# A two-layer graph kernel on one core: a chunk's semaphore is raised by a drain on TensorE in place of a product

## The chip, the cores and the metric
One core of one Trainium2 chip. The metric is the device time of the whole kernel in microseconds (us), the median over runs. TensorE is called PE in the profile (PEld its weight loads), VectorE DVE, ScalarE ACT, GpSimd POOL, SyncE SP.

## The reference
Two graph layers over 6250 nodes of 512 features and 106250 edges (`src`, `dst`), each followed by a layer norm:

```
x_l = x @ W_l.T + b_l                                   # layer 0
agg = segment_sum(x_l[src], dst);  deg = segment_sum(1, dst)
x   = layernorm(x + agg / max(deg, 1) + x @ W_r.T)
msg = h[dst] @ W_neigh.T + b_neigh                      # layer 1, h = x
neigh = segment_sum(msg, src) / max(deg, 1)
out = relu(h @ W_self.T + b_self + neigh)
x   = layernorm(x + layernorm(h + out) * gamma + beta)
```

The kernel sums the neighbours' rows first and multiplies by the weights afterwards, so the heavy part of each layer is: for each edge gather one row of 512 features and add it to the sum of its node.

## The kernel before
Nodes are cut into T = 49 tiles of 128. A layer's edges are cut into 928 chunks of 128 edges that all fall in one tile; two chunks make a group. For one chunk:

- POOL (`gathers`, L351 to L367) fetches the 128 rows from a table in HBM by an indirect DMA into one of GB = 8 slots of `rows`. A table row is a high and a low fp16 half with its scale. Before it reuses a slot it waits for `s_mm` of the chunk eight back (L363).
- DVE (`hot`, L563) builds `onehot`, the 128x128 matrix that says which row belongs to which node of the tile, once the rows have landed.
- PE (`sums`, L771) multiplies `onehot` with the two halves (two products of 512 columns) and with a column that counts edges (one product of 1 column). That last product raises `s_mm`.
- DVE (`add`, L572) adds a finished group from PSUM to `acc` in SBUF, some groups behind, after a wait for `s_mm` (L579), and raises `s_acc`. PE may start a group only when the sums of two groups back (layer 0) or four groups back (layer 1) have been added.

Chunks are handled in Python loops of U = 16 inside a hardware loop. In layer 1 the roles of `src` and `dst` are exchanged, so its edges must be sorted by the other end. That is done beside the first 832 chunks of layer 0, one column (`placed`) per chunk: DVE writes `spot` and `where` (`spots`, L585), ACT scales `spot` into `put1` and `put2` (`puts`, L851), and PE multiplies the two with `where` in four products of 464 columns (`place`, L747), the last of which raises `placed`. `spot`, `put` and `where` have PB = 4 slots, so DVE (L595) and ACT (L857) wait for `placed` of the column four back. On PE a chunk's column goes ahead of its sums.

The stages in order of time: preparation and the table of layer 0 (to about 520 us of the span), the 832 chunks with a placed column (to 1830), the last 96 chunks of layer 0 (to 1970), the projections and the norm of layer 0 (to 2350), the 928 chunks of layer 1 (to 3720), the projections and the norms of layer 1.

Of the kernel before, what the change touches and what calls it, by code (L numbers as in the profile page):

```python
# [18 lines left out]
def gnn_two_layers(nc, x, src, dst, w_l_t, b_l, w_r_t, w_self_t, b_self, w_neigh_t, b_neigh, gamma, beta, out):  # L19
# [12 lines left out]
    EC = -(-(-(-E // P)) // U) * U  # L32
# [18 lines left out]
    PB = 4  # L51
# [10 lines left out]
    with ctx:  # L62
# [122 lines left out]
        s_mm = sem("s_mm")  # L185
# [55 lines left out]
        @block.sync  # L241
        def _(sp):
            sp.wait_ge(s_pad, 3)
            for a, given in enumerate((src, dst)):
                sp.dma_start(edges[0:EFULL, a, :], given[0:EFULL * EC].rearrange("(p c) -> p c", c=EC)).then_inc(s_edges, 16)
                sp.dma_start(edges[EFULL:EFULL + 1, a, 0:EREST],
                             given[EFULL * EC:E].rearrange("(p c) -> p c", p=1)).then_inc(s_edges, 16)
            sp.dma_start(dst_next[0:EFULL, :], dst[1:EFULL * EC + 1].rearrange("(p c) -> p c", c=EC)).then_inc(s_edges, 16)
            sp.dma_start(dst_next[EFULL:EFULL + 1, 0:EREST - 1],
                         dst[EFULL * EC + 1:E].rearrange("(p c) -> p c", p=1)).then_inc(s_edges, 16)  # L250
            for a, given in enumerate((src, dst)):
                n = WP * WIN
                for b in range(WB - 1):
                    sp.dma_start(win_i[a][:, b, :], given[b * n:(b + 1) * n].rearrange("(p j) -> p j", j=WIN)).then_inc(s_wins, 16)
                sp.dma_start(win_i[a][0:WP - 1, WB - 1, :],
                             given[(WB - 1) * n:(NWIN - 1) * WIN].rearrange("(p j) -> p j", j=WIN)).then_inc(s_wins, 16)
                sp.dma_start(win_i[a][WP - 1:WP, WB - 1, 0:WREST],
                             given[(NWIN - 1) * WIN:E].rearrange("(p j) -> p j", p=1)).then_inc(s_wins, 16)
            for k in range(4):
                sp.dma_start(acc[:, k * XG:(k + 1) * XG, 0:D],  # L260
                             x[k * XG * P:(k + 1) * XG * P, :].rearrange("(t p) d -> p t d", p=P)).then_inc(s_x[k], 16)
            sp.dma_start(acc[0:LAST, T - 1, 0:D], x[(T - 1) * P:N, :]).then_inc(s_x[4], 16)

            with sp.Fori(0, T // BATCH) as i:
                for k in range(BATCH):
                    sp.wait_ge(s_high, BATCH * i + k + 1)
                    sp.wait_ge(s_low, BATCH * i + k + 1)
                    sp.wait_ge(s_tail, BATCH * i + k + 1)
                    sp.dma_start(tables[0][ds((BATCH * i + k) * P, P), :], rows[:, k, :]).then_inc(s_tab[k], 16)
            for layer in range(2):  # L270
                wa, wb = ((w_l_t, w_r_t), (w_neigh_t, w_self_t))[layer]
                if layer:
                    sp.wait_ge(s_proj, T)
                else:
                    sp.wait_ge(lists[1]["placed"], EC)
                    for n, a in enumerate((b_l, b_self, b_neigh, gamma, beta)):
                        sp.dma_start(vec[n], a.rearrange("(o d) -> o d", o=1).to_broadcast([P, D])).then_inc(s_vec, 16)
                sp.dma_start(w_a[:], wa.rearrange("(k p) n -> p k n", p=P)).then_inc(s_w, 16)
                sp.dma_start(w_b[:], wb.rearrange("(k p) n -> p k n", p=P)).then_inc(s_w, 16)
                source = (x, h_dram)[layer]  # L280
                target = (h_dram, out)[layer]

                def load(t, k, n=P):
                    sp.dma_start(own[0:n, k, :], source[ds(t * P, n), :] if not isinstance(t, int)
                                 else source[t * P:t * P + n, :]).then_inc(s_own[k], 16)

                def tile(t, k, load_next=True):
                    n = LAST if layer == 1 and isinstance(t, int) and t == T - 1 else P
                    sp.wait_ge(s_res, layer * T + t + 1)
                    rows_of = (lambda a: a[t * P:t * P + n, :]) if isinstance(t, int) else (lambda a: a[ds(t * P, n), :])  # L290
                    sp.dma_start(rows_of(target), res[0:n, k % 2, :]).then_inc(s_st[k % 2], 16)
                    if layer == 0:
                        sp.dma_start(rows_of(tables[1]), res_tab[0:n, k % 2, :]).then_inc(s_st[k % 2], 16)
                    if not isinstance(t, int) or t + OB < T:
                        last = isinstance(t, int) and t + OB == T - 1
                        load(t + OB, k, LAST if last and layer == 0 else P)

                sp.wait_ge(s_mm, chunk0(layer) + CHUNKS[layer])
                for t in range(OB):
                    load(t, t)  # L300
                over_tiles(sp, tile)
            for k in range(2):
                sp.wait_ge(s_st[k], stored(1, T - 1 - (T - 1 - k) % 2, k))
# [70 lines left out]
        def _(dve):  # L374
# [141 lines left out]
            def unpack(layer):  # L516

                s, n = lists[layer], CHUNKS[layer]
                dve.wait_ge(s["placed"], EC)
                halves = "p (h c) -> p h c"  # L520
                v2i, v2h = (flat[:, k * 1024:k * 1024 + n].bitcast(i32) for k in (0, 1))
                link(V.tensor_copy(v2i.rearrange(halves, h=2), ps[:, 2:4, 0:n // 2]))
                link(V.tensor_scalar(v2h, v2i, 8, None, ALU.arith_shift_right))
                link(V.scalar_tensor_tensor(g_idx[layer][:].rearrange(halves, h=2), ps[:, 0:2, 0:n // 2], 8.0,
                                            v2h.rearrange(halves, h=2), ALU.mult, ALU.add))
                link(V.tensor_scalar(v2h, v2i, 255, None, ALU.bitwise_and))
                link(V.tensor_scalar(g_loc[layer][:], v2h, -1.0, None, ALU.add))
# [57 lines left out]
            def spots(i, k, first):  # L585

                s, col = lists[1], U * i + k
                if k == 0:
                    if not first:
                        dve.wait_ge(s["where"], U * i)  # L590
                    V.tensor_copy(lo_ring[:], lo[:, ds(U * i, U)])
                    V.tensor_copy(hi_ring[:], hi[:, ds(U * i, U)]).then_inc(s_ring, 1)
                    dve.wait_ge(s_ring, i + 1)
                if not (first and k < PB):
                    dve.wait_ge(s["placed"], col - PB + 1)  # L595
                V.tensor_scalar(spot[:, k % PB, :], iota_node[:], lo_ring[:, k:k + 1], None,  # L596
                                ALU.is_equal).then_inc(s["spot"], 1)
                V.tensor_scalar(where[:, k % PB, 0:CHUNKS[1]], iota_chunk[:, 0:CHUNKS[1]], hi_ring[:, k:k + 1], None,  # L598
                                ALU.is_equal).then_inc(s["where"], 1)
# [108 lines left out]
        def _(pe):  # L708
# [38 lines left out]
            def place(layer, col, k, start=False, stop=False):  # L747
                s, half = lists[layer], CHUNKS[layer] // 2
                pe.wait_ge(s["where"], col + 1)
                if layer:  # L750
                    pe.wait_ge(s["put"], col + 1)
                for n, put in enumerate((put1, put2)):
                    for b in range(2):
                        last = mm(ps[:, 2 * n + b, 0:half], put[:, k % PB, :],
                                  where[:, k % PB, b * half:(b + 1) * half], start=start, stop=stop)
                last.then_inc(s["placed"], 1)

            pe.wait_ge(s_flag, 3)
            flag = pe.value_load(unsorted[0:1, 0:1], min_val=0, max_val=1)
# [11 lines left out]
            def sums(layer, i, first=False, placing=None):  # L771
                g = GROUP[layer]
                for k in range(U):
# [7 lines left out]
                    if k % g == 0 and not (first and q < 2):  # L781
# [4 lines left out]
                    mm(ps[:, bank, :], lhs, row[:, D:2 * D], start=False, stop=stop)  # L786

                    mm(ps[:, bank + 1, 0:1], lhs, row[:, 2 * D + 2:2 * D + 4].bitcast(bf16)[:, 0:1],
                       start=start, stop=stop).then_inc(s_mm, 1)

            for layer in range(2):
                iters = CHUNKS[layer] // U
# [42 lines left out]
        def _(act):  # L835
# [15 lines left out]
            def puts(c, first=False):  # L851
                s = lists[1]
                for k in range(PB):
                    col = PB * c + k
                    act.wait_ge(s["spot"], col + 1)
                    if not first:
                        act.wait_ge(s["placed"], col - PB + 1)  # L857
                    nc.scalar.activation(put1[:, k, :], spot[:, k, :], ACT.Copy, scale=val1[:, ds(col, 1)])  # L858
                    nc.scalar.activation(put2[:, k, :], spot[:, k, :], ACT.Copy,  # L859
                                         scale=val2[:, ds(col, 1)]).then_inc(s["put"], 1)  # L860
# [59 lines left out]
```

## Time and profile before

| | us |
|---|---|
| median of 3 runs | 4253.43 (4247.24 to 4258.62) |
| the profiled execution | 4222.63 |
| its span | 4220.8 |
| PE busy in the span | 2795.4 |
| DVE busy | 2605.4 |
| POOL busy | 1896.1 |
| ACT busy | 813.8 |

The span runs from the first to the last instruction of the profiled execution. Shares of busy time are averages over stages with different limits; each stage has to be read by itself.

### The profile page before, as it was taken

The page shows a single profiled execution, that of the slowest core. Times are in us where ns is not written, and L with a number is a line of the kernel's source. Part 1 is how long each engine was busy: PE and PEld are TensorE (multiplying, and loading weights), DVE is VectorE, ACT ScalarE, POOL GpSimd, SP SyncE. Part 2 cuts the span into 40 slices and gives each one's busy share as a digit, 9 for nine tenths or more (in the row PEclk, how much of TensorE's full clock was granted, in tenths as well). Part 3 has the DMA queues.
Part 4 walks back from the last instruction along what each step waited for, and adds up shares of the span by engine and source line. Part 5 has one row for each costly group of instructions (what it writes and reads, how often), then busy time and mean ns, then how long its engine had stood idle before and what let it go on. Part 6 is the DMA issues. An engine that isn't in the chain of part 4 may idle for free.

```text
span 4220.8 us, 57125 instructions
## 1 busy us (share of the span) xinstructions
PE 2795.4 (66%) x11308; PEld 1186.1 (28%) x11308; DVE 2605.4 (62%) x6523; ACT 813.8 (19%) x2156; POOL 1896.1 (45%) x2073
## 2 busy tenths in 40 slices
PE   1000088888888888866999655555555555568887
PEld 1000033333333433322554211111111111124443
DVE  3878877777777777754555444444444444448887
ACT  0300044444444444410222000000000000002222
POOL 0600066666666666664000366666666666630000
PEclk9555599999999999976999766666566665669999
DMA  3300066666666666664333566666666666661111
GB/s 141 123 0 0 21 169 165 170 165 167 167 169 166 168 167 167 168 202 137 102 103 98 160 178 173 179 179 179 177 178 174 180 177 177 172 115 60 55 60 50
DMA packets 201222, 586.38 MB, mean 139 GB/s; under 512 B 34672, under 2 KB 35502, under 8 KB 201196
## 3 DMA queue, kind: packets, MB, share of 16 engines
q0 software_dynamic: 148480, 488.56, 42.6%
q1 hardware_dynamic: 52716, 97.53, 7.1%
q8 instruction: 10, 0.16, 0.0%
q14 instruction: 16, 0.13, 0.0%
HBM read 534.51 MB, written 51.44 MB: 139 GB/s over the span
## 4 chain that ended last, share of the span: by engine, by line
PE 38%; DVE 19%; issue 19%; DMA 8%; DVEq 6%; POOL 2%; another core or an unknown queue 2%; ACT 2%; SPq 2%; POOLq 0%; ACTq 0%
PE ps L710 37%; DMA rows<-table,idx_ring 7%; DVEq L576 4%; DVE acc L583 3%; DVE onehot L569 2%; POOL rows L364 2%; DVE flat L501 2%; DVE flat L502 1%; DVE flat L503 1%; DVE where L598 1%; PE ps L812 1%; DVE st L658 1%; DVE spot L596 1%; PE ps L815 1%
## 5 line engine op out<-in xcount | busy, mean ns | idle before, releaser
L364 POOL DMA_INDIRECT rows<-table,idx_ring x1856 | 1793.8, 966 | 1394.7 <-issue 462.6
L710 PE MATMUL ps<-rows,onehot 128*128 128x512 f16 (+1 forms) x5568 | 1393.7, 381 | 758.0 <-DVE onehot L569 346.3
L583 DVE TENSOR_TENSOR acc<-acc,ps 128x513 f32 x928 | 638.2, 688 | 830.5 <-issue 353.7
L710 PE MATMUL ps<-where,put 128*128 128x464 f16 x3328 | 805.5, 365 | 348.8 <-ACT put L859 291.4
L710 PEld LDWEIGHTS ps<-rows,onehot 128*128 128x128 bf16 x5568 | 526.5, 111 | 1650.1 <-issue 888.2
L569 DVE TENSOR_SCALAR onehot<-iota_node,loc_ring,rows 128x128 bf16<-128x128 f16 x1856 | 586.4, 323 | 297.6 <-DMA rows<-table,idx_ring 253.1
L858 ACT ACTIVATE put<-spot,flat 128x128 f16<-128x128 f16 x832 | 334.1, 402 | 1091.7 <-DVE spot L596 860.7
L710 PEld LDWEIGHTS ps<-where,put 128*128 128x128 f16 x3328 | 268.1, 98 | 659.2 <-issue 351.8
L598 DVE TENSOR_SCALAR where<-iota_chunk,hi_ring 128x928 f16<-128x928 f16 x832 | 378.8, 455 | 0.0
L872 ACT ACTIVATE flat<-acc,rdeg 128x512 f32 (+1 forms) x98 | 69.4, 710 | 1551.2 <-DVE rdeg L647 1547.6
L710 PE MATMUL ps<-w_a,flat 128*128 128x512 f32 x784 | 356.0, 597 | 0.1
L710 PE MATMUL ps<-w_b,flat 128*128 128x512 f32 x784 | 352.4, 592 | 0.0
L859 ACT ACTIVATE put<-spot,flat 128x128 f16<-128x128 f16 x832 | 321.0, 386 | 0.6 <-issue 0.6
L596 DVE TENSOR_SCALAR spot<-iota_node,lo_ring 128x128 f16<-128x128 f16 x832 | 210.0, 252 | 28.0 <-PE ps L710 17.2
L710 PEld LDWEIGHTS ps<-w_b,flat 128*128 128x128 f32 x784 | 149.0, 190 | 187.5 <-issue 187.5
L345 POOL COPY acc<-zeros 128x513 f32 (+1 forms) x49 | 34.4, 703 | 344.3 <-ACT flat L872 344.3
L710 PEld LDWEIGHTS ps<-w_a,flat 128*128 128x128 f32 x784 | 142.8, 192 | 144.0 <-issue 143.1
L891 ACT ACTIVATE sd<-mv,eps 128x1 f32<-128x1 f32 x147 | 43.3, 295 | 626.8 <-DVE mv L663 626.8
L679 DVE SCALAR_TENSOR_TENSOR flat<-where,has,ps 128x512 f32<-128x512 f32 x49 | 36.6, 747 | 133.1 <-PE ps L710 133.1
L710 PE MATMUL ps<-totals,ones 128*128 128x49 f32 x2 | 0.7, 430 | 160.3 <-DVE flat L480 160.3
L658 DVE BATCH_NORM_STATS2 st<-flat 128x6 f32<-128x512 f32 x147 | 102.1, 695 | 5.0
L812 PE MATMUL ps<-ident,flat 128*128 128x128 f32 x392 | 62.3, 283 | 59.9 <-ACT flat L881 49.1
(131 smaller groups left out, 1361.9 us busy)
## 6 DMA issues: line engine op xcount, KB each, us to landing
rows<-table,idx_ring POOLq DMA_INDIRECT x1856
table<-rows SPq DMA_DIRECT2D x98, 257.0 KB, 3.2
h_scratch<-rows SPq DMA_DIRECT2D x49, 256.0 KB, 2.0
rows<-h_scratch SPq DMA_DIRECT2D x49, 256.0 KB, 2.7
acc<-in_x SPq DMA_DIRECT2D x4, 3072.0 KB, 23.5
rows<-in_x SPq DMA_DIRECT2D x48, 256.0 KB, 3.2
out<-rows SPq DMA_DIRECT2D x48, 256.0 KB, 2.0
w_a<-in_w_l_t SPq DMA_DIRECT2D x1, 1024.0 KB
```

The source lines that it names most:

```text
L364: nc.gpsimd.indirect_dma_start(out=rows[:, k % GB, :], out_offset=None, in_=tables[layer][:, :], in_offset=bass.IndirectOffsetOnAxis(ap=id ...
L501: link(V.tensor_tensor_scan(run, mask[:], mask[:], base[:, ds(b, 1)], ALU.add, ALU.bypass))
L569: V.tensor_scalar(onehot[:, k % SB, :], iota_node[:], loc_ring[:, k:k + 1], rows[:, k % GB, 2 * D:2 * D + 2].bitcast(f32), ALU.is_equal, A ...
L576: tile = dve.value_load(g_tile[layer][0:1, ds(U // g * i + q, 1)], min_val=0, max_val=T - 1)
L583: V.tensor_tensor(tile_acc, tile_acc, part, ALU.add).then_inc(s_acc, 1)
L596: V.tensor_scalar(spot[:, k % PB, :], iota_node[:], lo_ring[:, k:k + 1], None, ALU.is_equal).then_inc(s["spot"], 1)
L598: V.tensor_scalar(where[:, k % PB, 0:CHUNKS[1]], iota_chunk[:, 0:CHUNKS[1]], hi_ring[:, k:k + 1], None, ALU.is_equal).then_inc(s["where"], 1)
L658: V.bn_stats(st[:], dest).then_inc(v, 1)
L710: return nc.tensor.matmul(*args, skip_group_check=True, **kw)
L812: nc.tensor.transpose(ps[:, 0, j * P:(j + 1) * P], mean_nb[:, k % 2, j * P:(j + 1) * P], ident[:])
L858: nc.scalar.activation(put1[:, k, :], spot[:, k, :], ACT.Copy, scale=val1[:, ds(col, 1)])
L859: nc.scalar.activation(put2[:, k, :], spot[:, k, :], ACT.Copy, scale=val2[:, ds(col, 1)]).then_inc(s["put"], 1)
```

## The change
A product no longer raises `s_mm`. After the three products of a chunk PE executes a drain, and the drain raises `s_mm`. Since PE's stream has the placed column of a chunk ahead of its sums, the drain stands for that column too: `placed` of layer 1's list is dropped, and DVE, ACT and SP wait for `s_mm` in its place, with the same number. No product, vector instruction or transfer is added, dropped or put in another order; 1856 drains are added. The branch for unsorted edges (`bin_column`), which these inputs do not take, keeps its own `placed`.

```diff
@@ sync
-                    sp.wait_ge(lists[1]["placed"], EC)
+                    sp.wait_ge(s_mm, EC)
@@ vector, unpack
-                dve.wait_ge(s["placed"], EC)
+                if layer:
+                    dve.wait_ge(s_mm, EC)
+                else:
+                    dve.wait_ge(s["placed"], EC)
@@ vector, spots
                 if not (first and k < PB):
-                    dve.wait_ge(s["placed"], col - PB + 1)
+                    dve.wait_ge(s_mm, col - PB + 1)
@@ tensor, place
-                last.then_inc(s["placed"], 1)
+                if layer == 0:
+                    last.then_inc(s["placed"], 1)
@@ tensor, sums
                     mm(ps[:, bank + 1, 0:1], lhs, row[:, 2 * D + 2:2 * D + 4].bitcast(bf16)[:, 0:1],
-                       start=start, stop=stop).then_inc(s_mm, 1)
+                       start=start, stop=stop)
+                    nc.tensor.drain().then_inc(s_mm, 1)
@@ scalar, puts
                     if not first:
-                        act.wait_ge(s["placed"], col - PB + 1)
+                        act.wait_ge(s_mm, col - PB + 1)
```

## Rows read from the trace of the kernel before

**Rows 1.** Windows, one row per stage: busy us and count of each engine, clock, DMA
```profile
core 0: us, PE busy (x) PEld busy (x) DVE busy (x) ACT busy (x) POOL busy (x), PEclk, DMA share, GB/s
530.00:1820.00 1290.00, 1094.26 (x5739) 500.14 (x5738) 957.30 (x3183) 569.82 (x1644) 812.96 (x821) 0.98 0.62 167
1840.00:1950.00 110.00, 64.08 (x223) 21.69 (x222) 48.60 (x131) 0.00 (x0) 68.79 (x73) 0.59 0.66 193
2430.00:3700.00 1270.00, 733.39 (x2568) 238.27 (x2567) 557.69 (x1496) 0.00 (x0) 810.11 (x857) 0.62 0.64 177
```

**Rows 2.** Groups by line and form, window 2430 to 3700 (layer 1's chunks)
```profile
L364 POOL DMA_INDIRECT rows<-table,idx_ring x857 | 810.5, 946 | 460.1 <-issue 212.0 <-PE ps L710 140.5 <-remote 107.6
L710 PE MATMUL ps<-rows,onehot 128*128 128x1 bf16 x856 | 169.5, 198 | 0.0
```

**Rows 3.** Timeline of layer 0 with columns, the steady rhythm: start, us, engine, instruction
```profile
1506.06 0.94 PE L710 MATMUL ps<-where,put 128*128 128x464 f16 x4
1506.84 0.60 PE L710 MATMUL ps<-rows,onehot 128*128 128x512 f16 x3
1507.30 0.94 PE L710 MATMUL ps<-where,put 128*128 128x464 f16 x4
```

**Rows 4.** Timeline of layer 0 with columns, a stop of all engines
```profile
1496.03 0.60 PE L710 MATMUL ps<-rows,onehot 128*128 128x512 f16 x3
...
1496.49 0.94 PE L710 MATMUL ps<-where,put 128*128 128x464 f16 x4
1496.83 0.94 POOL L364 DMA_INDIRECT rows<-table,idx_ring  x1 [0.37 <-issue]
1499.11 0.69 DVE L583 TENSOR_TENSOR acc<-acc,ps 128x513 f32 x1 [3.50 <-remote]
...
1499.74 0.94 POOL L364 DMA_INDIRECT rows<-table,idx_ring  x1 [1.98 <-remote]
...
1499.86 0.61 PE L710 MATMUL ps<-rows,onehot 128*128 128x512 f16 x2 [2.42 <-DVE acc L583]
```

**Rows 5.** Timeline of layer 1's chunks, another such stop
```profile
2607.09 0.98 POOL L364 DMA_INDIRECT rows<-table,idx_ring  x1 [0.30 <-issue]
...
2608.57 0.31 DVE L569 TENSOR_SCALAR onehot<-iota_node,loc_ring,rows 128x128 bf16<-128x128 f16 x1
...
2608.93 0.61 PE L710 MATMUL ps<-rows,onehot 128*128 128x512 f16 x3 [0.95 <-issue]
2609.17 0.94 POOL L364 DMA_INDIRECT rows<-table,idx_ring  x1 [1.10 <-PE ps L710]
...
2611.89 1.03 PE L710 MATMUL ps<-rows,onehot 128*128 128x512 f16 x3 [2.35 <-DVE onehot L569]
2612.05 0.94 POOL L364 DMA_INDIRECT rows<-table,idx_ring  x1 [1.93 <-remote]
```

**Rows 6.** Timeline of layer 0's norm: a product ends, DVE starts
```profile
2049.79 2.31 PE L710 MATMUL ps<-w_b,flat 128*128 128x512 f32 x5
...
2052.25 0.75 DVE L679 SCALAR_TENSOR_TENSOR flat<-where,has,ps 128x512 f32<-128x512 f32 x1 [2.60 <-PE ps L710]
```

**Rows 7.** Waits, window 530 to 1820: us in total, times, longest
```profile
POOL rows L364 <- PE ps L710: 221.8, 143, 2.4
DVE acc L583 <- PE ps L710: 156.3, 108, 3.4
DVE acc L583 <- remote: 91.4, 30, 3.7
```

**Rows 8.** Chain that ended last, by line, windows 530 to 1830 and 2360 to 3710
```profile
by line: PE ps L710 57.5%; issue 12.3%; DVE acc L583 6.2%; another core or an unknown queue 5.2%; DVE where L598 3.8%; DVEq L576 3.5%; DVE onehot L569 3.4%; DVE spot L596 2.6%; ACT put L859 1.9%; DVEq L583 0.5%; DVE idx_ring L560 0.4%; ACT 
by line: issue 34.3%; PE ps L710 19.7%; DMA rows<-table,idx_ring 17.7%; DVEq L576 7.8%; POOL rows L364 6.5%; DVE onehot L569 3.6%; DVE acc L583 3.5%; another core or an unknown queue 1.9%; DVEq L583 1.2%; DVEq L578 0.9%; DVEq L579 0.7%; DVE
```

**Rows 9.** The page's second part: granted clock of PE in 40 slices
```profile
PEclk9555599999999999976999766666566665669999
```

## The prediction
> **What bounds the kernel now.** I read the windows by stage first, then the timelines of two stretches, then the waits and the chain. The windows [rows 1] give three stages that the change touches. With placed columns, 821 gathers start in 1290 us, so a chunk takes 1.571 us; in the last 96 chunks of layer 0 it takes 110/73 = 1.51 us; in layer 1 1270/857 = 1.482 us. No engine is full in any of them: PE is busy 85% of the first and 58% of the last, POOL 63% and 64%, DVE 74% and 44%, and the DMA engines 62 to 66%.
>
> Two floors can be read. POOL needs 0.946 us for a gather in layer 1 [rows 2] and 0.99 with columns (812.96 us for 821 [rows 1]), and its queue adds 0.30 us between two when nothing else is waited for (the gather at 2607.09 [rows 5]). That makes about 1.25 and 1.29 us. PE, in the steady rhythm with columns, goes from one chunk's first placing product at 1506.06 to the next one's at 1507.30 [rows 3]: 1.24 us, with the clock at its upper level (0.98 granted [rows 1]). So 0.28 to 0.33 us of every chunk with columns, and 0.23 us of every chunk of layer 1, are stops.
>
> The stops have a form that the timelines show. At 1497.43 (1496.49 + 0.94) PE has ended all it may do; it waits for a DVE add. That add waits for a product that PE finished before 1497.43, yet it starts only at 1499.11, after 3.50 us of idle whose end the profile puts down to "remote", that is, to nothing that it knows. POOL's last gather ended at 1497.77 and it waits till 1499.74 [rows 4]. For 1.3 us nobody works, and the one event that can end it is PE's semaphore. In layer 1 PE's last product ends at 2609.54 (2608.93 + 0.61), and POOL, free since 2610.11, starts its next gather at 2612.05, again by "remote" [rows 5]. In the norm, where POOL gathers nothing, the same kind of signal is prompt: products that end at 2052.10 release DVE at 2052.25 [rows 6]. I read this as: **while gathers run, the semaphore that a product raises can arrive 1 to 3 us after the product has ended**, and DVE's signals to PE do not (an onehot that ends at 2608.88 lets PE start at 2608.93 [rows 5]). With columns POOL and DVE wait 222 + 156 + 91 us for PE or "remote" [rows 7], in part at the same time; in layer 1 POOL alone waits 140.5 + 107.6 us [rows 2].
>
> **The change part by part.** *The drain's price on PE.* No row has a drain in such a place. PE must let the last product end before it starts the next. That product is the one-column one; a mean of 0.198 us in layer 1 [rows 2], and today the next product starts about 0.03 us behind it (the seven products start at seven places in 1.24 us: four by 0.195, two by 0.215, the rest of 0.03 is the one-column product [rows 3]). Lost overlap: 0.17 - 0.03 = 0.14 us at the upper clock, taking the one-column product at 0.17 there, which is an estimate from 0.198 for a mostly lower clock. After it the queue must start again; a semaphore-to-product restart takes 0.05 us [rows 5], and the drain itself and the wait instruction behind it are of that size each. Estimate 0.25 us per chunk; bounds 0.14 (the overlap alone) and 0.45 (0.14 plus a restart as slow as POOL's 0.30).
>
> *What hides it.* With columns PE's rhythm becomes 1.24 + 0.25 = 1.49, still under the 1.571 of today. In layer 1, where the clock is mostly at the lower level (0.62 granted [rows 1]), PE needs 733.39/857 = 0.86 us per chunk, with a drain some 1.1, under POOL's 1.25. So the drain is covered in both, if the stops go away; if they stay, PE's share of the chain (57.5% [rows 8]) grows with it.
>
> *The drain's semaphore.* The new signal is raised by PE's queue after the engine is empty, and not by the product. I take it to be prompt. That is the choice on which the forecast stands, and no row shows it; what speaks for it is that products pile up behind the late signal (PE works on for up to three chunks after the product that the add waits for), so it is the message that is late and not the work, and that the signals of the other engines are not late in the same microseconds [rows 4, 5].
>
> A page of the Trainium skill can be laid beside this. Perfetto Trace Analysis, sections "Tensor Engine Instruction" and "Sequencer-only Instruction (DRAIN, etc)", lets a product's update be pushed once PSUM has acknowledged the writes, and a drain's by the sequencer: another route, which is what the forecast needs, though no run here shows whether it is a faster one. PSUM — Partial Sum Buffer, section "Engine vs sequencer instructions", says to put the increment on the product itself, since it fires on completion, and that a drain waits for the engine to go fully idle. By that rule nothing is late today and the drain only costs (the first rival below). The norm agrees with it, the stop at 1499.11 does not.
>
> *The dropped signal.* DVE's `spots` and ACT's `puts` now wait for the whole chunk four back and not for its column alone: 0.46 us later (1507.30 - 1506.84 [rows 3]) plus the drain. Behind that wait in DVE stand onehot and the add, behind ACT's the next `put`. The slots are four chunks deep, 6 us, so I cost it at nothing; if DVE's lead over PE is gone it is up to 0.5 us per stop. SP's weight loads start 0.5 us later, beside the 96 chunks: nothing. One update fewer per chunk on PE: nothing, no row prices it.
>
> *The sum, chosen.* With columns a chunk goes from 1.571 to 1.53 (PE's 1.49 and a rest for DVE's and POOL's own unevenness): 832 x 0.04 = 33 us saved. Bounds: with a drain at 0.14, PE 1.38, chunk 1.42, 125 saved; at 0.45, PE 1.69, chunk 1.69, 100 lost. Last 96 chunks: half of the way from 1.51 to 1.25: 12 saved. Layer 1: the way from 1.482 to POOL's 1.25 is 0.23; I take half, since DVE's queue and the landings stop POOL too (DVEq, issue and DMA hold most of the chain [rows 8]): 928 x 0.12 = 111 saved; bounds 0 and 0.21, 195. Norms and preparation: 0. Together 33 + 12 + 111 = 156 us. The profiled execution took 4222.6, so 4067 by its own time; the median of the runs lies 31 us above it (4253.4), so I give 4097 as the time. Ends of this case: -340 and about 0.
>
> *The clock.* It is at the upper level while PE works without pause and mostly at the lower one in layer 1 [rows 9]. Here PE's products per microsecond do not fall if the chunk does not get longer, so I give it nothing.
>
> **The rivals.**
> 1. *The drain mends nothing.* Its semaphore is as late as the product's, or the product's was never late. The stops stay, and each chunk on PE's part of the chain pays the drain: 0.575 x 1300 = 748 us [rows 8] are 603 chunks of 1.24, times 0.25 = 150; in layer 1 0.197 x 1350 = 266 us, about 300 chunks of 0.86, of which a fall of 0.15 each would be 45. Some is given back because PE runs dry less often; I take 150 in all: 4253 + 150 = 4403. It decides once lateness gives back less than about 0.1 us per chunk. For it: the rhythm has only 0.33 us of slack. Against it: signals of other engines come in time.
> 2. *The drain itself is held until the late message is out.* Then PE can't work on in a stop: per stop (138 waits of DVE with columns [rows 7], about 130 of POOL in layer 1) two chunks are done after it and not in it: 138 x 2 x 1.24 = 342, 130 x 0.86 = 112: 4253 + 450 = 4700. Against it: one would expect the message, not the engine, to be stuck.
> 3. *It comes out even.* The drain costs 0.45 us, with columns 100 us are lost, layer 1 gives 111 back: 4253 - 11 = 4242. Or what ends the stops is a gather's landing and not PE's semaphore, and the drains are all covered: also about 4250. Against: PE waits in [rows 4] with all its inputs there but the add.
>
> **How the numbers follow.** Forecast 0.51, rival 1 0.27, rival 2 0.12, rival 3 0.10. Within 0.3% (13 us, about what a measurement of this kernel can tell from no change) is half of rival 3 and a little of the edges: 0.06. Faster: the forecast and a fifth of rival 3, 0.53. Slower: 0.41. The time is that of the likeliest, 4097; its own range is 3990 to 4210. The range that leaves 0.1 below and the second rival above reaches from 3990 to 4450.
>
> **What would show it.** In the profile after: stops ended by "remote" gone from DVE's add and POOL's gather with columns and in layer 1; gathers per microsecond in layer 1 up, 1.36 us per chunk; with columns PE's rhythm 1.49 and not 1.24 and few waits of PE for the add. The forecast is wrong if "remote" waits stay (rival 1), if PE stands between a product's end and the next start for over 1 us again and again (rival 2), or if the rhythm with columns is over 1.57 (rival 3).

## The result, and the profile after

| | before | after |
|---|---|---|
| median of 4 runs, us | 4254.04 (4247.24 to 4258.62) | 4426.99 (4418.61 to 4428.11) |
| the profiled execution | 4222.63 | 4428.11 |
| its span | 4220.8 | 4426.3 |

The changed kernel takes 1.0404 of the time of before [1.0385, 1.0423]: 173 us more, where 156 us less were forecast. The profile of before (4222.63) lies outside the range of its four runs and inside that of chip 2 below (4214.22 to 4224.43), and the record doesn't say on which chip it was taken. So the two profiles differ by 205.5 us where the medians differ by 173, and up to 33 us of what follows by stage need not be the change's. The profiles put the loss in the stages that the change touches. First the page of the changed kernel: its busy times, the granted clock (answers to [rows 9]) and, from the fifth part, the two groups that wait longest for PE's queue.

```profile
PE 3019.8 (68%) x11308; PEld 1192.7 (27%) x11308; DVE 2708.9 (61%) x6523; ACT 813.2 (18%) x2156; POOL 1869.2 (42%) x2073
...
PEclk9555699999999999995799955555555555559999
...
L364 POOL DMA_INDIRECT rows<-table,idx_ring x1856 | 1766.8, 952 | 1624.4 <-PEq L794 833.5
...
L586 DVE TENSOR_TENSOR acc<-acc,ps 128x513 f32 x928 | 640.1, 690 | 786.5 <-PEq L794 545.0
```

L794 is the drain. Then the windows by stage (they answer to [rows 1]): busy us and count of each engine, clock, DMA share.

```profile
540.00:1900.00 1360.00, 1074.85 (x5401) 475.15 (x5400) 986.89 (x2990) 535.01 (x1544) 740.82 (x772) 0.99 0.55 149
1950.00:2040.00 90.00, 64.51 (x269) 23.61 (x268) 50.13 (x145) 14.55 (x42) 53.92 (x58) 0.76 0.69 205
2560.00:3870.00 1310.00, 886.90 (x2569) 241.13 (x2570) 572.20 (x1499) 0.00 (x0) 809.36 (x857) 0.50 0.62 172
```

Gathers per window give the time of a chunk: with placed columns 1360/772 = 1.762 us (was 1.571), in layer 1 1310/857 = 1.529 (was 1.482), in the last 96 chunks of layer 0 90/58 = 1.55 (was 1.51). Times 832, 928 and 96 that is +159, +43 and +4 us: 206 us, the difference of the spans (205.5). The other stages lose nothing.

The waits of the stage with columns (us in total, times, longest; answers to [rows 7]):

```profile
POOL rows L364 <- PEq L794: 540.0, 654, 2.4
DVE acc L586 <- PEq L794: 309.1, 339, 3.8
```

"Remote" is gone, as forecast. But the two engines now wait more often, for PE's queue. The timeline of the same place as [rows 3 and 4] shows why:

```profile
1490.61 0.94 PE L713 MATMUL ps<-where,put 128*128 128x464 f16 x4 [0.33 <-ACT put L864]
...
1491.09 0.94 POOL L364 DMA_INDIRECT rows<-table,idx_ring  x1 [0.81 <-PEq L794]
...
1491.39 0.60 PE L713 MATMUL ps<-rows,onehot 128*128 128x512 f16 x3
...
1492.16 0.69 DVE L586 TENSOR_TENSOR acc<-acc,ps 128x513 f32 x1 [0.97 <-PEq L794]
...
1492.32 0.94 PE L713 MATMUL ps<-where,put 128*128 128x464 f16 x4 [0.32 <-issue]
...
1492.80 0.94 POOL L364 DMA_INDIRECT rows<-table,idx_ring  x1 [0.76 <-PEq L794]
```

PE's rhythm is 1492.32 - 1490.61 = 1.71 us where it was 1.24. The stops of 2 to 3 us are gone, and every chunk has a pause of 0.33 us instead. The trace's records of PE's queue split the 0.49 us from the start of the one-column product to the next product's start (medians): 0.19 until the drain has ended, 0.10 more until a register instruction starts, 0.09 until the wait on the next chunk's inputs, 0.08 until the weight load, 0.03 until the product. Without the drain the whole way took 0.03. So **a drain costs 0.46 us a chunk with columns**, and 0.30 of it comes after the drain has ended, while the queue starts again from empty.

In layer 1 (records again) the next product starts 0.43 to 0.55 us after the one-column product's start, where before it took about 0.07, and there most chunks are held by it: chunks follow each other every 1.25 or 1.35 us on PE, at or above POOL's 1.25. And a new kind of stop stands there (timeline, answers to [rows 5]):

```profile
2988.88 1.03 PE L713 MATMUL ps<-rows,onehot 128*128 128x512 f16 x3 [0.22 <-issue]
...
2991.39 0.13 PEld L713 LDWEIGHTS ps<-rows,onehot 128*128 128x128 bf16 x2 [1.97 <-issue]
2991.40 1.03 PE L713 MATMUL ps<-rows,onehot 128*128 128x512 f16 x3 [1.49 <-issue]
2991.60 0.69 DVE L586 TENSOR_TENSOR acc<-acc,ps 128x513 f32 x1 [0.69 <-PEq L794]
...
2991.86 0.94 POOL L364 DMA_INDIRECT rows<-table,idx_ring  x1 [1.46 <-PEq L794]
```

The products end at 2989.91, and the next chunk's inputs have been there for long (in the median a onehot is done 6.9 us ahead of its last product). Still PE, DVE and POOL start only at 2991.4 or after: by its record the drain ended 1.38 us after the one-column product's start. It was held. In the records of 870 chunks of layer 1, 15% of the drains end over 0.4 us after the one-column product's start (normally 0.24; at the 95th percentile 1.99), 178 us too much in all. With columns it is 0.9% of them.

### The profile page after: what moved, and what is told of

The parts are those of the page before. It is cut to its first block, busy times and chain, and to the rows that moved or that the text cites. A ratio compares the mean times of both kernels' runs of the same rounds, so it can differ in the third digit from the quotient of the medians.

```text
span 4426.3 us, 58981 instructions
## 1 busy us (share of the span) xinstructions
PE 3019.8 (68%) x11308; PEld 1192.7 (27%) x11308; DVE 2708.9 (61%) x6523; ACT 813.2 (18%) x2156; POOL 1869.2 (42%) x2073
## 4 chain that ended last, share of the span: by engine, by line
issue 33%; PEldq 21%; DVE 17%; PE 13%; PEld 6%; DMA 3%; ACT 3%; DVEq 2%; SPq 2%; ACTq 1%; POOL 0%; POOLq 0%
PEldq L794 19%; PE ps L713 11%; PEld ps L713 6%; DVE acc L586 2%; DVE flat L501 2%; DMA rows<-table,idx_ring 2%; ACT put L864 2%; DVE spot L599 2%; DVE flat L502 1%; DVE flat L503 1%; DVE where L601 1%; PE ps L817 1%; DVE st L661 1%; PE ps L820 1%; DVE onehot L572 1%
## 5 line engine op out<-in xcount | busy, mean ns | idle before, releaser
L364 POOL DMA_INDIRECT rows<-table,idx_ring x1856 | 1766.8, 952 | 1624.4 <-PEq L794 833.5
L713 PE MATMUL ps<-rows,onehot 128*128 128x512 f16 (+1 forms) x5568 | 1562.7, 406 | 529.2 <-issue 445.8
L713 PE MATMUL ps<-where,put 128*128 128x464 f16 x3328 | 794.3, 361 | 558.5 <-ACT put L864 357.3
L572 DVE TENSOR_SCALAR onehot<-iota_node,loc_ring,rows 128x128 bf16<-128x128 f16 x1856 | 623.1, 338 | 441.2 <-DMA rows<-table,idx_ring 423.1
L601 DVE TENSOR_SCALAR where<-iota_chunk,hi_ring 128x928 f16<-128x928 f16 x832 | 394.2, 474 | 0.0
```

The costliest lines, as they stand in the source:

```text
L364: nc.gpsimd.indirect_dma_start(out=rows[:, k % GB, :], out_offset=None, in_=tables[layer][:, :], in_offset=bass.IndirectOffsetOnAxis(ap=id ...
L572: V.tensor_scalar(onehot[:, k % SB, :], iota_node[:], loc_ring[:, k:k + 1], rows[:, k % GB, 2 * D:2 * D + 2].bitcast(f32), ALU.is_equal, A ...
L713: return nc.tensor.matmul(*args, skip_group_check=True, **kw)
```

## The experiments

Chips differ, and this has to be known for all that follows. On the chip of the result and on chips 14, 13 and 2 (it may be one of them, the record gives it no number) the kernel before takes 4218 to 4255 us; on chips 12, 7, 0 and 1 it takes 3780 to 3785. The ratios of times are all within one chip. I read each trace's records of semaphore updates against the ends of the products that raise them. "Late" is over 60 ns behind. The shares are of the updates that are on record: in chip 12's trace all of them are, in the profile of before 684 of 820 with columns and 648 of 856 in layer 1. An update is set against the last product that ended ahead of it, so the real lateness can only be larger.

```
s_mm of the kernel before / without `placed`   late with columns   late in layer 1   us per chunk
the profile of before                          72%                 56%               1.571 / 1.482
chip 12 (e2)                                   0                   0                 1.306 / 1.259
chip 2 (e18)                                   78%                 62%               1.577 / 1.480
```

In the profile of before half of the recorded signals come over 0.68 us late with columns (worst 2.6 us), in layer 1 the worst is 6.0. In the same windows DVE's and ACT's signals come 8 to 13 ns after the end, as on chip 12 (only half to three quarters of them are on record, though), and PE's come within 15 ns in the norm of layer 0. So the forecast's reading of the stops held: where signals are prompt, the very same program takes 11% less time, and its chunks run at POOL's floor of 1.25 to 1.3 us.

One thing beside the late signals also differs, and the forecast had no term for it. In layer 1 of the profile of before 286 instructions of DVE's own queue, nearly all of which otherwise take 0.02 to 0.06 us, took about 0.7, 178 us in all (289 and 179 us on chip 2, none on chip 12). DVE's queue stands on the chain of that stage [rows 8], so a part of layer 1's stops is DVE's and not PE's; no run parts the two. In the changed kernel 45 are left.

**The drain without its signal.** Before, with a bare drain behind each chunk's products, which raises nothing.

```diff
                        start=start, stop=stop).then_inc(s_mm, 1)
+                    nc.tensor.drain()
```

> The kernel before, with a drain that raises nothing behind the three products of every chunk; the one-column product still raises s_mm and the placed column its own semaphore. It asks whether the route of the signal matters or only the pause and the slower pace that the drain brings. Theory A (the route: a signal raised by a drain is prompt, one raised by a product is late while gathers run): POOL's start after the end of the one-column product of eight chunks back stays spread over 2.4 to 5.6 us as before, and the time is above that of the changed kernel, 4440 to 4550 us, since the drain's price (0.46 us per chunk with columns) is paid and the lateness too. Theory B (the pause: lateness goes because PE stops after each chunk and POOL no longer runs back to back with columns): the same 0.80 us as after the change, and the time of the changed kernel, 4410 to 4440 us.

> The kernel of the first experiment again (a drain that raises nothing behind every chunk; the products raise the semaphores). Where signals are prompt it must equal the changed kernel within 0.3%, as the drain's pause is all that counts. On a chip with lateness it parts route from pause: by theory A (route) the products' signals stay late and it is slower than the changed kernel by 1% or more, by theory B (pause and slower pace) equal to it.

Chip 12: 4178.59 us against 3780.48, 1.1052 [1.1034, 1.1071]. Chip 7: 4185.11 against 3784.94, 1.1058 [1.104, 1.1077]. A chunk takes 1.720 us with columns and 1.319 in layer 1 (1.306 and 1.259 without): 832 x 0.414 + 928 x 0.060 = 400 of the 398 us. The price of the drain is there with no change in who signals. The second expectation was missed: it put this kernel within 0.3% of the changed one, which takes 0.6% more (4210.96, below). Whether the pause or the signal's route cures lateness could not be told on chips that have none.

**The dropped signal alone.** The products raise `s_mm` as before; `placed` is dropped and its waits go to `s_mm`.

```diff
-                    dve.wait_ge(s["placed"], col - PB + 1)
+                    dve.wait_ge(s_mm, col - PB + 1)
...
-                last.then_inc(s["placed"], 1)
+                if layer == 0:
+                    last.then_inc(s["placed"], 1)
...
-                        act.wait_ge(s["placed"], col - PB + 1)
+                        act.wait_ge(s_mm, col - PB + 1)
```

> One part of the change alone: the semaphore placed is dropped and DVE, ACT and SP wait for s_mm in its place, but s_mm is still raised by the one-column product and there is no drain. Theory A (what costs is the drain on PE): within 0.5% of the kernel before, 4235 to 4275 us. Theory C (the later release of the placed column's slots costs): slower by 1 to 2%, 4300 us or more. Theory D (PE's signals are late because there are two per chunk to deliver): faster, 4150 to 4220 us, with fewer waits that nothing explains.

> The part of the change without drains (placed dropped, the one-column product raises s_mm), again, for a chip with lateness. Theory D (fewer signals of PE, less lateness): faster than the kernel before by 1% or more there, with fewer late signals than 72%. Theory A (the number does not matter): within 1%, with 60 to 80% of the signals with columns late. On a chip without lateness 1.000 again.

> placed dropped alone, a third time, for the same purpose. On a chip with lateness, theory D: faster by 1% or more; theory A: within 1%. On a chip without it 1.000 again.

1.000 [0.999, 1.0009] on chip 12, 0.9999 [0.9989, 1.0008] on chip 1, and on chip 2, where signals are late, 1.0006 [0.9996, 1.0016]. Half as many updates per chunk with columns leave 78% of the rest late. The windows of chip 12's run, with columns and in layer 1, show what the program does with prompt signals. The second window runs past the last gather at 3305 us, so its 714 gathers took 905 us, 1.27 each:

```profile
560.00:1600.00 1040.00, 1004.29 (x5578) 485.77 (x5576) 939.96 (x3089) 551.89 (x1592) 794.74 (x797) 1.00 0.73 202
...
2400.00:3400.00 1000.00, 723.95 (x2365) 232.47 (x2364) 544.36 (x1360) 19.70 (x43) 674.75 (x714) 0.63 0.71 193
```

**Fewer drains.** One drain per group of two chunks, which raises `s_mm` by 2; `placed` is dropped here too, as in all that follows on `s_mm`.

```diff
+                    if k % g == g - 1:
+                        nc.tensor.drain().then_inc(s_mm, g)
```

> The changed kernel, with one drain per group of two chunks that raises s_mm by 2, so half as many drains. If the drain's price is 0.46 us on PE with columns and 0.36 to 0.45 in layer 1, half of it goes: with columns PE's rhythm goes from 1.70 to 1.47 us per chunk, in layer 1 from 1.30 to about 1.08. Theory A (PE's rhythm is the bound after the change in both stages): 150 to 190 us less with columns and 60 to 130 us less in layer 1, in all 4130 to 4220 us, under the kernel before. Theory E (in layer 1 it is the held drains and not PE's rhythm): only the part with columns is won, 4240 to 4280 us.

> The kernel with one drain per group of two chunks, again, for a chip with lateness. PE's rhythm with columns is 1.47 us per chunk, so gathers are again issued more closely. Theory P: as the pace comes near that of the gathers lateness returns in part; 4180 to 4280 us, about the kernel before. Theory A' (half the drains give the whole relief): 4050 to 4180 us, under the kernel before. On a chip without lateness 3940 us again.

Chip 12: 3939.04, 1.042 [1.0403, 1.0437]; 1.500 us with columns, 1.261 in layer 1, where it costs nothing. Half of the drains cost about half: 0.19 of the 0.43 of the changed kernel (1.734 against 1.306). Chip 13, where signals are late: 4341.55 against 4254.75, one run each, above both of its expectations; 1.680 and 1.520. By the records 47% of its drains with columns end over 0.4 us after the one-column product's start (none on chip 12), 125 us too much over 760 chunks, 0.165 a chunk: that and chip 12's 1.500 are 1.665 of the 1.680. In layer 1 it is 35%. In the changed kernel, with a drain after every chunk, 0.9% and 15% were held: in these two kernels, the more products stand between two pauses, the more drains are held.

**Drains in layer 0 alone.** The change as it is, but in layer 1 the one-column product raises `s_mm`.

```diff
+                    (nc.tensor.drain() if layer == 0 else count).then_inc(s_mm, 1)
```

> Drains in layer 0 alone; in layer 1 the one-column product raises s_mm as before. It parts the loss by layer. From the traces (1.571 to 1.762 us per chunk with columns, 1.482 to 1.529 in layer 1) 160 us of the loss belong to layer 0 and 44 to layer 1 of the profiled execution: 4254 + 130 to 165 = 4385 to 4420 us, with layer 1 at 1.48 us per chunk. A rival: the traces of single executions mislead and layer 1 is where the loss is: 4300 us or less.

Chip 12: 4137.15, 1.0942 [1.0924, 1.096]; 1.734 us with columns, 1.260 in layer 1. Of the change's loss there some 357 us are layer 0's.

**The change itself where signals are prompt, and with a second drain.**

```diff
                        start=start, stop=stop)
+                    nc.tensor.drain()
                     nc.tensor.drain().then_inc(s_mm, 1)
```

> The changed kernel itself, once more. The first four experiments ran on a chip on which the kernel before takes 3780 us and not 4254, and on which every signal of a product arrives within 20 ns. Theory F (a drain costs PE 0.46 us per chunk everywhere, and it is only the lateness, where a chip has it, that pays a part back): on a chip without lateness the ratio is 1.10 to 1.11, about 4180 us against 3780; on one with lateness it is 1.04 again. A rival: the ratio is 1.04 on every chip, and the difference of the chips is something that meets both kernels alike.

> The changed kernel with a second drain, which raises nothing, ahead of the one that raises s_mm. It splits the 0.46 us: what is the wait for the last product to end is paid once, what is the drain's own handling is paid twice. If the wait and the restart of the weight load and product are most of it: PE's rhythm with columns goes up by 0.02 to 0.10 us, the time by 20 to 100 us over the changed kernel on the same chip. If it is the drain's own handling: by 0.2 us or more, 200 us or more.

Chip 7: the change takes 4210.96 against 3784.94, 1.1128 [1.111, 1.1147], 426 us more; 1.734 and 1.334 us a chunk, and no drain longer than 0.24 us. That the drain carries the signal costs 26 us over the silent one (4185.11). Two drains take 4349.54, 1.1498 [1.1479, 1.1517]: the second adds 0.076 us from product to product, and 1.812 and 1.412 us a chunk (0.078 each). So of the first one's 0.46 only some 0.08 is what one more drain adds; the rest, lost overlap and the restart, is paid once per pause.

**No drain, one signal per group.** `last` is the one-column product.

```diff
+                    if k % g == g - 1:
+                        last.then_inc(s_mm, g)
```

> No drain; placed dropped; the one-column product of the second chunk of each group raises s_mm by 2 and that of the first chunk nothing: a quarter of the signals with columns, half in layer 1. Theory D (late signals come of too many): on a chip with lateness faster than before by 1% or more, without lateness within 0.5% or up to 1% slower, since slots come free two at a time. Theory A (number does not matter): within 1% or slower on either.

> One signal per group, raised by 2 by the one-column product of the group's second chunk, no drain, placed dropped, again, for a chip with lateness: a quarter of the signals with columns and half in layer 1. Theory D: 1 to 4% faster than the kernel before there. Theory A: equal, or 1 to 3% slower, since a late signal now holds back two slots. On a chip without lateness 0.999 again.

> One signal per group by the second chunk's product, no drain, placed dropped, a third time, to find it on a chip with lateness (the kernel before above 4200 us). Theory D (fewer signals, less lateness): 1 to 4% faster than the kernel before there. Theory A: equal, or 1 to 3% slower, since a late signal holds back two slots. On a chip without lateness 0.998 again.

0.9989 [0.998, 0.9999] on chip 7, 0.9984 [0.9974, 0.9993] on chip 1, and 1.0028 [1.0016, 1.0039] on chip 2, where 78% of the recorded signals with columns are still late. With lateness it is no cure, without it it gives 4 or 5 us. So the number of signals is not the cause.

**Memory traffic of its own.** SP copies pieces of `x` inside HBM beside the chunks of both layers, one after the other; the kernel's result doesn't use them.

```diff
+            def traffic(done):
+                for i in range(150):
+                    sp.dma_start(bg[0:512, :], x[0:512, :]).then_inc(s_bg, 16)
+                    sp.wait_ge(s_bg, 16 * (i + done + 1))
```

> The kernel before with foreign traffic: SP copies the first 512 rows of x (1 MB) to a scratch in HBM, 150 times beside layer 0's chunks and 150 times beside layer 1's, one at a time. It asks whether a product's signal becomes late when the memory is loaded by someone else, on a chip where it is prompt. Theory G (lateness comes from load on the memory and the DMA engines): signals of products in the chunk stages arrive up to microseconds after the end, waits that nothing explains appear, the time is over 4100 us. Theory H (load on them does nothing to the signals; the lateness comes from elsewhere on the chip): the gathers get slower, the chunks wait for landings, and every signal of a product still arrives within 20 ns of its end; 3850 to 4300 us.

> The same with small copies: 64 rows (128 KB), 300 times in each layer, one at a time. Theory G: a small number of late signals, 3800 to 3950 us. Theory H: none, and the time within 1% of the kernel before on the same chip, as the gathers leave the DMA engines a quarter of their time.

> The changed kernel with the traffic of 1 MB copies. Theory G: the drains give back a part of the lateness, and it stands at a ratio of 1.02 to 1.07 to the kernel before with the same traffic, not at 1.11. Theory H: where both wait for landings the drains' price is partly covered by them, the ratio lies between 1.03 and 1.10 with no late signal and no drain held longer than 0.27 us after the last product's start.

One run each on chip 0. With 1 MB pieces before takes 3928.78 (3782.29 without), 1.420 and 1.322 us a chunk at a DMA share of 0.92 and 330 GB/s, and not one product signal is late; with pieces of 64 rows the time does not move (3782.29). The changed kernel with the large pieces takes 4235.01 (1.078 of before with them) and no drain is held. On this chip more traffic than on any late one does not make PE's signals late; on a late chip it was not tried.

**The silent drain where signals are late.** The kernel of the first experiment on chip 14.

> The kernel with a drain that raises nothing, a third time, to find it on a chip on which the kernel before takes about 4254 us. There, by theory A (route), the signals of its products are late as before and it takes 4440 us or more; by theory B (the pause and the slower pace), its signals are prompt with columns and it takes 4380 to 4440 us. On a chip on which the kernel before takes 3780 us it must take 4180 us again and tells nothing new.

4397.29 against 4218.34, one run each (1.042, as the change itself). Product signals are now late in 1.2% of the chunks with columns and 20.8% of those of layer 1, although they take the old route; and 15.3% of layer 1's drains are held, some 180 us in all, as in the changed kernel. So it is the pause that makes signals prompt, and not the drain's route. This trace has both records for 561 chunks of layer 1. Where the drain was held (115), the product's signal was late in 114, in two thirds of them 33 ns ahead of the drain's end, in the others 0.7 or 1.4 us ahead; where it was not (446), in 2, and the signal again 32 to 34 ns ahead of the drain's end. **A drain is held where the product's signal is late, and it never ended before that signal.** Most of these drains end with the signal; the rest are held for one or two more steps of 0.7 us, the same length that DVE's queue shows. Two chunks of its timeline with columns, for PE:

```profile
1490.93 0.94 PE L710 MATMUL ps<-where,put 128*128 128x464 f16 x4 [0.31 <-issue]
...
1491.71 0.60 PE L710 MATMUL ps<-rows,onehot 128*128 128x512 f16 x3
...
1492.62 0.94 PE L710 MATMUL ps<-where,put 128*128 128x464 f16 x4 [0.31 <-issue]
```

**A slower PE without a pause.** In place of a drain, four extra products of 512 columns ahead of each group's first one, with columns only; the first real product overwrites what they leave.

```diff
+                    if placing is not None and start:
+                        for _ in range(4):
+                            mm(ps[:, bank, :], lhs, row[:, 0:D], start=True, stop=False)
```

> The kernel before, without drains and with placed, with four extra products of 512 columns in each group of layer 0's chunks with columns (they write what the group's first product then overwrites, so nothing else changes). PE's rhythm there goes from 1.24 to 1.24 + 2 x 0.215 = 1.67 us per chunk, near the drains' 1.70, but PE never pauses. Theory P (pace: signals are late where gathers are issued back to back, and a slower chunk alone ends it): on a chip with lateness less than 10% of the signals with columns come late, a chunk takes 1.67 to 1.75 us, the time is 4300 to 4400 us. Theory Q (pause: PE must empty for its signals to get out): over half of the signals stay late with columns and a chunk takes 1.8 us or more, 4450 us or more. On a chip without lateness both give 1.68 to 1.70 us per chunk and 4090 to 4120 us.

```profile
540.00:1840.00 1300.00, 1300.00 (x6991) 625.46 (x6990) 933.40 (x3012) 538.51 (x1554) 759.00 (x778) 1.00 0.58 158
```

Chip 13: 4320.02 against 4254.75, one run each; 1.672 us a chunk with columns, and PE is busy for the whole of the window. 57.6% of the signals are late still (median 0.16 us, 95th percentile 1.17, worst 1.72), though the chunks come slower than before (1.57 in the profile of before; chip 13 has no trace of that kernel). They cost nothing there, since PE never ran dry: of theory Q the late signals came and the 1.8 us a chunk did not. A slower pace alone does not make the signals prompt; the pauses with an empty pipe do, mostly.

## Why the prediction was wrong

It came out on the other side. By the prediction's own steps:

- *The stops are late signals of PE's products while gathers run*: right in the main on this kind of chip, by the records of updates and by the same program on chips where none is late; in layer 1 a part of them may be the 0.7 us instructions of DVE's queue. That the 1.25 and 1.29 us of POOL are the floors: right, chips with prompt signals run at 1.259 and 1.306.
- *The drain's price on PE, 0.25 us, bounds 0.14 to 0.45*: too small, and the first cause. It measured 0.46 with columns, just outside the upper bound, and some 0.4 in layer 1. The lost overlap was about right (0.16 for 0.14). What follows was put at three steps of 0.05 (drain, wait, restart), which with 0.14 add up to 0.29 and not to the 0.25 that was taken; a register instruction, a wait, a weight load and the product follow one another there, 0.30 together. PE's rhythm is therefore 1.70 and not 1.49, and PE bounds the stage: 1.734 us a chunk where nothing is late, 1.762 here, against the 1.53 of the sum. Of the 192 us by which this stage missed its term by the profiles (+159 for -33), 832 x (1.734 - 1.53) = 170 are the price.
- *"I take it to be prompt"; "it is the message that is late and not the work"*: this is the step that failed in kind. The drain's signal is no more prompt than the product's by its route. What makes the product's signal late holds the drain as well (114 of 115 held drains), and a drain waits with PE's queue stopped. That the change made signals prompt with columns is the work of its pause, and it bought that at a price above the stops. In layer 1 the forecast's 1.36 us would have been nearly right without held drains: the changed kernel takes 1.334 on chip 7. Here 178 us over 870 chunks, 0.20 a chunk, come on top: 1.54, measured 1.529. That turned -111 into +43. It is rival 2's mechanism, in layer 1 alone. That rival had priced it at 112 us, with one chunk done late per stop where its own sentence says two.
- *"So the drain is covered in both"*: it was covered in neither, since in layer 1 PE's rhythm became 1.25 to 1.35 and not 1.1.
- *The dropped signal costs nothing*: right (1.000, 0.9999, 1.0006).
- *The clock gives nothing*: in layer 1 it was granted 0.50 instead of 0.62, the lower of its two levels throughout, where before it stood at the upper one at times. A part of the 1.334 may be this; no run separates it.
- *The ends of the sum, "-340 and about 0", and the range 3990 to 4210*: the terms' own bounds, 100 lost with columns and 0 in layer 1, make an upper end of 100 lost, about 4353. It was left out of the range. The result lies beyond even that, by the higher price with columns and by the held drains, for which the sum had no term.

Of the rivals, the first had the nearest time (4403) by a mechanism that is half right: it kept the stops and added a drain of 0.25 on a part of the chunks, whereas the stops went and a drain of 0.46 fell on all. Rival 3's 0.45 us for the drain was the right size, and only the gain in layer 1 beside it was not there. Where signals are prompt the rule weighed in the prediction, from the Trainium skill's page PSUM — Partial Sum Buffer, section "Engine vs sequencer instructions", agrees with the result: 0% late, and the drain only costs (1.1128). On the late chips its sentence that a product's update fires on completion can hold too, if completion itself is late there; no run shows that.

What stays open is why the signals of products come late and drains are held on some chips and not on others, and why in the stages with gathers and not in the norms. Fewer signals and a slower pace of PE did not cure it, and more traffic did not bring it on where it is absent; a gather-free or slowed-gather version of the kernel was not run, nor more traffic on a late chip. No version here beats the kernel before on both kinds of chips.

## What to carry to other kernels

A drain in a stream of products costs the restart of the queue more than itself, so count every instruction between the drain and the next product one after the other, and set that against the slack of PE's rhythm before anything else. A late semaphore is not mended by moving it to another instruction that is held by the same cause; measure first, with a silent copy of the instruction, whether its route or its pause does the work. Time a change that aims at waits on more than one chip: here the same edit costs 4% on one and 11% on another, and the time of the program itself differs by 12%.

## What the runs showed of the hardware

- A drain between products: 0.46 us from product to product with the clock at its upper level (0.99 granted), about 0.4 in layer 1 (0.50 granted); a second one right behind it 0.076.
- Without drains 56 to 78% of the recorded `s_mm` updates of a product come over 60 ns late in the stages with gathers, in the profile of before (up to 2.6 us with columns and 6.0 in layer 1) and on chip 2. With columns PE's late updates often come out in groups of 5 to 8, mostly 50 to 60 ns apart (some 120 such groups). On chips 12, 7, 0 and 1 no update is late. On chip 14 only a kernel with drains was traced.
- On the late chips other queues are held up too. In the profile of before DVE's queue has the 286 instructions of about 0.7 us in layer 1, and with columns some 50 register instructions of ACT's took 0.7 instead of 0.04; on chip 12 there is none.
- On chip 0 traffic of 330 GB/s at a DMA share of 0.92 leaves every product signal prompt.
